# Macaron block on one core: GpSimd's rounding, subtraction and weight spreading cut into smaller instructions

## The reference, cut to what matters

```python
x = x + 0.5 * ffn(layernorm(x), ...)          # first FFN
x = x + attention(layernorm(x), Wq, .., memory_keys, memory_values)
x = x + 0.5 * ffn(layernorm(x), ...)          # second FFN, same weights

# ffn: 4096 tokens of width 128, 8 experts, the best 2 of each token, hidden width 176
scores = sigmoid(x @ gate_w.T); sel = top_k(scores + expert_bias, 2)
# routed: token times its score, bf16 products, square(relu(x @ up_e.T)) @ down_e.T, summed over the 2
# shared: square(relu(x @ shared_up.T)) @ shared_down.T, in fp32

# attention: 4096 keys and values of width 128, fp32
q = x @ Wq.T + bq
out = softmax(q @ memory_keys.T / sqrt(128)) @ memory_values @ Wo.T + bo
```

## Time and profile before

| | |
|---|---|
| median of three runs | 636.55 us (635.56 to 638.65) |
| profiled execution | 636.61 us, its span 634.8 us |
| TensorE clock granted | full in all of the span |
| PE busy | 599.1 us (94%) |
| DVE busy | 528.3 us (83%) |
| ACT busy | 454.0 us (72%) |
| POOL busy | 415.5 us (65%) |
| first FFN | about 0 to 111 us of the span |
| second FFN | about 544 us to the end |

### The profile page before, as it was taken

The page is one execution under the profiler, slowest core; times in us unless marked ns, Lnnn a source line. Parts: engine busy times, 40 slices in busy tenths (PEclk is TensorE's granted clock), DMA queues, the critical chain, the costliest instruction groups (busy, mean ns, idle before and its releaser), DMA issues.

```text
span 634.8 us, 10665 instructions
## 1 busy us (share of the span) xinstructions
PE 599.1 (94%) x3508; PEld 443.4 (70%) x3508; DVE 528.3 (83%) x913; ACT 454.0 (72%) x756; POOL 415.5 (65%) x484
## 2 busy tenths in 40 slices
PE   7799989899899999999999999999999999899987
PEld 3466656567677777777877778777787767566655
DVE  5899886988977978978887897897888858899884
ACT  3577776576777867767777776776877786488886
POOL 4868980564476865966768687596678887536520
PEclk9999999999999999999999999999999999999999
DMA  8012120425447274473744727446374460000001
GB/s 310 13 34 68 35 68 1 128 65 124 117 99 172 56 170 106 95 162 75 161 99 103 169 60 170 106 94 158 76 162 89 115 133 1 1 2 35 36 18 50
DMA packets 36118, 59.28 MB, mean 93 GB/s; under 512 B 9312, under 2 KB 9952, under 8 KB 35936
## 3 DMA queue, kind: packets, MB, share of 16 engines
q1 hardware_dynamic: 31808, 52.82, 33.9%
q10 hardware_dynamic: 3744, 4.74, 3.0%
q0 software_dynamic: 512, 1.05, 0.6%
HBM read 8.25 MB, written 2.10 MB: 16 GB/s over the span
## 4 chain that ended last, share of the span: by engine, by line
PE 57%; DVE 16%; POOL 10%; issue 9%; SPq 3%; ACT 3%; ACTq 0%; DMA 0%; POOLq 0%; DVEq 0%
PE banks L1501 7%; PE banks L1502 7%; PE banks L1503 7%; PE banks L1546 7%; PE banks L1548 7%; PE banks L1547 7%; PE banks L1525 4%; DVE bank_max L1218 4%; SPq L387 3%; DVE E L1213 3%; POOL xn L524 3%; DVE probsT L1100 2%; PE banks L1556 2%; PE banks L1358 2%; PE banks L1343 1%
## 5 line engine op out<-in xcount | busy, mean ns | idle before, releaser
L612 POOL TENSOR_TENSOR p_lo<-probsT,p_hi 128x768 fp32r<-128x768 f32 (+1 forms) x128 | 226.7, 1776 | 119.6 <-ACT p_hi L822 119.1
L1218 DVE TENSOR_REDUCE bank_max<-banks 128x1 f32<-128x1024 f32 x128 | 155.9, 1219 | 30.5 <-PE banks L1503 29.7
L822 ACT ACTIVATE p_hi<-probsT 128x768 fp32r<-128x768 f32 (+1 forms) x128 | 104.4, 816 | 28.2 <-PE banks L1548 24.4
L1501 PE MATMUL banks<-kv_lo,q_parts 128*128 128x512 f32 x256 | 111.6, 436 | 4.1 <-ACT E L847 1.8
L1213 DVE STREAM_TRANSPOSE E<-E 128x1024 f32<-128x1024 f32 x92 | 113.5, 1234 | 0.4
L1100 DVE SCALAR_TENSOR_TENSOR probsT<-banks,E 128x1024 bf16<-128x1024 f32 x80 | 96.0, 1218 | 20.9 <-PE banks L1343 19.6
L847 ACT ACTIVATE E<-banks,neg_max 128x1024 f32<-128x1024 f32 x92 | 102.4, 1113 | 10.4 <-DVE neg_max L1224 8.0
L1546 PE MATMUL banks<-p_hi,kv_lo 128*128 128x512 f32 x256 | 107.6, 420 | 1.4 <-issue 1.1
L720 ACT ACTIVATE probsT<-probsT 128x1024 bf16<-128x1024 bf16 x96 | 92.1, 981 | 17.9 <-DVE probsT L1100 14.8
L1548 PE MATMUL banks<-p_hi,kv_hi 128*128 128x512 f32 x256 | 102.3, 400 | 0.0
L1547 PE MATMUL banks<-p_lo,kv_hi 128*128 128x512 f32 x256 | 102.2, 399 | 0.0
(11 more groups left out here) (133 smaller groups left out, 935.5 us busy)
## 6 DMA issues: line engine op xcount, KB each, us to landing
probsT<-E SPq DMA_DIRECT2D x208, 128.0 KB, 2.4
probsT<-E SPq DMA_DIRECT2D x232, 64.0 KB, 2.0
probsT<-E ACTq DMA_DIRECT2D x72, 64.0 KB, 2.1
E<-in_keys_values SPq DMA_DIRECT2D x8, 512.0 KB, 3.5
out<-X SPq DMA_DIRECT2D x8, 256.0 KB, 2.0
X<-in_x SPq DMA_DIRECT2D x1, 1280.0 KB, 9.0
probsT<-E POOLq DMA_DIRECT2D x16, 64.0 KB, 2.4
X<-in_x SPq DMA_DIRECT2D x3, 256.0 KB, 5.3
```

What stands on the lines that cost most here:

```text
L612: pool.tensor_tensor(moved_part(p_lo, ring), moved_pair(ring // UP, ring % UP), moved_part(p_hi, ring).bitcast(fp32), ALU.subtract).then_i ...
L822: act.activation(moved_part(p_hi, ring), moved_pair(ring // UP, ring % UP), ACT.Copy).then_inc(moved_hi_done, 1)
L1218: dve.tensor_reduce(bank_max[:, i % 2, h:h + 1], score_pair(u, i, h).rearrange("p b n -> p (b n)"), AX.X, ALU.max).then_inc(bank_max_done, 1)
L1501: pe.matmul(bank, qh, kl, start=True, stop=False)
```

## The change

The rounding of a block becomes eight instructions of 128 columns instead of one of 1024. The subtraction becomes eight of 128 instead of four of 256. Each subtraction now waits for the rounding of its own columns and no longer for the whole block, though all eight roundings come first in the stream. The spreading of weights, in both FFNs, is done in parts of 16 weights by 16 copies, that is 256 columns. A pair of groups takes four instructions instead of one, the single groups 0 and 1 two instead of one. Group 8's weights are spread by VectorE (L1009) and do not change.

```diff
+KV_PARTS = 8
@@ spread_weights
-                pool.tensor_copy(wide_weights(G)[:, slots, :].rearrange("p s (m r) -> p (s m) r", r=ROWS),
-                                 weight[:, slots, :, :].rearrange("p s t e -> p (s t e)").unsqueeze(2)
-                                 .to_broadcast([P, T * E, ROWS])).then_inc(weights_spread, 1)
+                wide = wide_weights(G)[:, slots, :].rearrange("p s (m r) -> p (s m) r", r=ROWS)
+                narrow = weight[:, slots, :, :].rearrange("p s t e -> p (s t e)").unsqueeze(2)
+                for m in range(0, T * E, 2 * E):
+                    last = pool.tensor_copy(wide[:, m:m + 2 * E, :],
+                                            narrow[:, m:m + 2 * E, :].to_broadcast([P, 2 * E, ROWS]))
+                last.then_inc(weights_spread, 1)
@@ ffn, f == 0
-                        pool.tensor_copy(kv_hi[:, i, :], kv_stage[:, i % 2, :]).then_inc(kv_hi_done, 1)
-                        pool.wait_ge(kv_hi_done, i + 1)
-                        for a in range(0, KVW, KVW // 4):
-                            part = slice(a, a + KVW // 4)
+                        for a in range(KV_PARTS):
+                            part = bass.ds(a * KVW // KV_PARTS, KVW // KV_PARTS)
+                            pool.tensor_copy(kv_hi[:, i, part], kv_stage[:, i % 2, part]).then_inc(kv_hi_done, 1)
+                        for a in range(KV_PARTS):
+                            part = bass.ds(a * KVW // KV_PARTS, KVW // KV_PARTS)
+                            pool.wait_ge(kv_hi_done, i * KV_PARTS + a + 1)
                             last = pool.tensor_tensor(kv_lo[:, i, part], kv_stage[:, i % 2, part],
                                                       kv_hi[:, i, part].bitcast(fp32), ALU.subtract)
                         last.then_inc(kv_lo_done, 1)
```

## The result

The changed kernel takes 640.01 us (median of 14 runs, 637.76 to 642.70), the kernel before 637.22 (median of 14 on the same chip, 634.71 to 638.80). The ratio is 1.0049, 95% interval 1.0028 to 1.0070. The forecast was 638.0, with 635.0 to 641.8 as its range. So it is slower by 2.8 us, twice the +1.45 of the forecast, and at the edge of the 0.5% that counts as no change. The profiled execution took 637.90 us with a span of 635.7, against 636.61 and 634.8 before.

The account below looks back on a forecast made before the run. TensorE sets even iterations and waits for VectorE, stalled by GpSimd, in odd ones; the change makes GpSimd the bound. First FFN +0.55 and second +0.9 give +1.45 us, so 638.0 us, range 635.0 to 641.8.

Parts of the forecast that it names:

- Iteration 1: First FFN: VectorE's stalls fall from 0.90 to about 0.4 us, so GpSimd starts the pair's weights 0.5 us earlier.
- The last hand-over: First FFN, third pair: GpSimd starts at 83.7, TensorE turns the weights at 85.95 instead of 85.38 us.
- The first FFN's sum: The first FFN ends 0.55 us later, with a GpSimd cycle of 22.5 us instead of 21.47.
- Group 0's 0.12: First FFN, iteration 0: spreading group 0's weights in two parts takes 0.12 us longer, paid in full.
- The steps of VectorE: First FFN: a sign to look for, VectorE's routing steps all under 0.5 us.
- What VectorE wins: First FFN: shorter stalls win about 1.1 us in each of iterations 3 and 5, becoming waiting on TensorE for GpSimd.
- The fixed cost of an instruction: GpSimd blocks: 11 more instructions at about 0.12 to 0.14 us each, less a 0.08 gap, add 1.26 us a block.
- Second FFN: Three pairs spread later by 0.36, 0.36 and 0.17 us, +0.9 us in all, with nothing won against it.
- its own case: The whole kernel: the forecast itself, a time of 637.0 to 639.7 us, chance 0.48.
- Pieces dearer: Rival: pieces cost more than the line, a block grows by 2.06 us or more, 641.8 to 644.3 us; chance 0.20.
- GpSimd keeps up: Rival: blocks grow little, GpSimd stays off the path and VectorE's gain comes through, 633.6 to 635 us; chance 0.13.
- The two effects cancel: Rival: the weights' lateness is smaller and partly taken up in odd iterations, 636 to 637 us; chance 0.19.

Follow-up runs that it names:

- filler_long: The kernel before, with four GpSimd memsets of 1024 columns added behind each of the blocks 0 to 4; 645.21 us, ratio 1.0121.
- again: The changed kernel run once more without any edit; 642.01 us, ratio 1.0073 to the kernel before.
- moved_eighths_whole: The changed kernel with one-copy spreading and blocks reordered: block 0 behind iteration 1, block 1 behind 3, six behind 5; 634.48 us, ratio 0.9968 to before.
- spread_whole: The changed kernel with the spreading of before, one copy, so only the blocks are in eighths; 637.72 us, ratio 1.0003 to before.
- spread_eighths: The kernel before, its blocks unchanged, with the spreading in parts of 128 columns; 641.32 us, ratio 1.0068.
- casts_eighths: The kernel before with only the rounding in eighths, subtractions in quarters behind one wait, spreading whole; 636.98 us, ratio 1.0001.
- subtract_eighths: The kernel before with only the subtraction in eighths, rounding and spreading whole; 637.46 us, ratio 0.9997.
- moved: The kernel before with blocks reordered: block 0 behind iteration 1, block 1 behind 3, six behind 5, same instructions; 632.53 us, ratio 0.9935.
- filler: The kernel before, with two GpSimd memsets (1024 and 512 columns) added behind each of the blocks 0 to 4; 637.30 us, ratio 1.0004.
- moved_eighths: The changed kernel with blocks reordered: block 0 behind iteration 1, block 1 behind 3, six behind 5; 636.56 us, ratio 0.9985 to before.
- blocks_as_before: The changed kernel with the blocks of before, so only the spreading is in parts; 638.85 us, ratio 1.0032 to before.

## Why the prediction came out as it did

- **What bounds.** It said that GpSimd would become the bound of the cycle, with the pairs at 38.7, 61.2 and 83.7. They start at 38.67, 61.20 and 83.71, without idle time before the last two. `filler_long` shows that GpSimd's length then passes to TensorE. Right for the cycle and for the turning of iteration 3. Of the signs it named, TensorE's idle time before L1323 came in iteration 3. In iteration 5 it is 0.17 us at most, because there VectorE is the last to come, as shown above.
- **Size of a piece and of the cycle.** 457, 287 and 395 ns were forecast, 454, 292 and 398 measured. The casts overlap less, so a block is 5.28 us and not 5.16, +1.38 instead of +1.26. The cycle is still 22.5 as forecast, because the gap of 0.08 put before the waiting instruction didn't come and some hundredths were saved at the joints. That the two errors cancel is luck.
- **Iteration 1, the first term that was mis-sized.** VectorE's stalls there fell from 0.90 to about 0.3 us, more than the forecast's 0.4. But from the turning of weights to the pair's start it is 38.67 - 30.01 = 8.66 us against 8.93, so of the 0.6 won on stalls 0.27 arrived, where the forecast counted 0.5. The start at 38.67 hides that: this profile stands 0.18 us earlier at the first mark than the one of before, where the forecast had it 0.12 later.
- **The last hand-over, the second.** Turnings were forecast at 63.45 and 85.95 and came at 63.50 and 86.17. The last weights are ready at 83.71 + 0.78 + 1.42 = 85.91, and TensorE starts 0.26 us behind them, not 0.05. The forecast took the weights for what releases this turning. It hangs on VectorE, and that its time was hit to 0.2 us is luck, because the two come almost together. The 0.21 us in rows 1 and 3 were no hand-over either: TensorE came to both turnings straight from its own products, so they were slack. Where TensorE really waits for the weights it starts 0.10 to 0.11 us behind them (40.98 and 63.50).
- **The first FFN's sum.** Between its two marks the forecast stands for +0.43 (its +0.55 less the 0.12 of group 0, ahead of the first mark). Measured were +0.99, and +1.06 in `again`. The two terms above, 0.23 and 0.21, are most of the gap. The first hand-over adds 0.07 (40.98 - 38.67 = 2.31 us against 2.24), the rest is roundings. By beats the +0.99 is 0.94 in iteration 3, 0.11 in each of the iterations 2 and 4, and -0.19 in iteration 5. Group 0's 0.12 is there: TensorE idles 0.44 us for the weights at 16.02, and 0.31 before.
- **The steps of VectorE.** That none would be over 0.5 us was wrong. The routing's first step, which adds 1 to the exponentials (TENSOR_SCALAR), now meets the longer block:

```profile
31.18 0.28 DVE L1048 TENSOR_TENSOR route<-route,best 128x64 f32<-128x64 f32 x1
...
50.42 0.68 DVE L1074 TENSOR_SCALAR route<-probs 128x64 f32<-128x64 f32 x1
...
55.62 0.45 DVE L1055 TENSOR_TENSOR route<-route,best 128x64 f32<-128x64 f32 x1
...
58.02 0.40 DVE L1051 TENSOR_TENSOR route<-route,rank 128x64 f32<-128x64 f32 x1
```

  The first step of the routing (50.42) stands for 0.48 us, until the subtractions of that block end (47.70 + 3.35 = 51.05). Ahead of the turning at 63.50 GpSimd sets the pace and it should cost little. The same stand at 72.95 lies on VectorE's way to the turning at 86.17. In `moved_eighths_whole` such a stand, with what follows from it, costs 0.68 per odd beat.
- **What VectorE wins.** The forecast counted about 1.1 us less stalling in each of the iterations 3 and 5. In iteration 3 it is 0.3: the stalls are 0.48 + 0.23 + 0.13 + 0.18 + 0.15 = 1.17 us against 1.49, since each is shorter but five steps are held up instead of three. Over the first FFN they fell from 3.80 to 2.63 us. This term was much too large. It did not reach the sum, which let all of that gain turn into waiting for GpSimd.
- **The fixed cost of an instruction.** A block grew by 1.38 us for 11 more instructions, 0.125 us each. The estimate from the Trainium skill, GPSIMD Engine Reference, section "Instruction dispatch" (0.46 us a block at 50 cycles each) would have kept GpSimd off the path; no run bears it out.
- **Second FFN.** +0.9 was forecast, as 0.36 + 0.36 + 0.17, and +1.03 measured. TensorE's beats give 0.38, 0.36 and 0.29 for the three pairs, so the last one is the term that was too small. For the first pair TensorE turns the weights 0.20 and the tokens 0.33 us later than in the earlier trace rows. `spread_whole` takes all of it back and `spread_eighths` brings +2.58.
- **Around the span.** Costed at nothing; it is +0.35. This step was missing from the sum altogether.
- **The time.** 640.01 us lies above the 637.0 to 639.7 that the forecast gave to its own case. The whole series of runs stood higher by 0.67 (the kernel before at 637.22 and not 636.55), and the rest is the effect, +2.8 where +1.45 was forecast. The path was right in the main, and the sum about half of what came.
- **The rivals.** *Pieces dearer* is out at its bounds (a block of 5.96) but points in the right direction. *GpSimd keeps up* is out for the whole change, since the idle time before L540 is gone; for half of it, `casts_eighths` and `subtract_eighths`, it holds, and what VectorE was to win there did not show in the medians. *The two effects cancel* holds for the blocks alone (`spread_whole`, 1.0003) and falls for the change, because nothing stands against the spreading.

With group 0's 0.12 that is 0.12 + 0.99 + 1.03 + 0.35 = 2.5 us of the 2.8 between the medians. The rest is below what they resolve: the interval of the ratio is 2.7 us wide.

## What to carry to other kernels

Cutting a GpSimd instruction so that VectorE gets in more often pays for every piece, here 0.12 to 0.14 us, on the engine whose slack per cycle (1.94 us) must hold them all. Count the pieces against that slack first, and never cut the instruction that another engine waits for as a whole. At each hand-over look whether the engine behind it stood idle for it: a product that is ready 0.21 us ahead is slack, not a wait. Where the work has no consumer for a long time, taking it out of the contended stretch (`moved`, -4.6 us between the medians, of them 3.2 in the first FFN) is worth more than making it finer.

## What the runs showed of the chip that was not expected

**Small pieces do not always let VectorE in.** Two-input steps mostly got in at the next boundary, 0.06 to 0.08 us after it. One waited out the rest of a train of eight casts (1.48 us). The TENSOR_SCALAR step with one input from SBUF waited for the end of the train each time it met one of subtractions or memsets (0.68 us in after, in `moved_eighths_whole` and in `filler`, 2.88 in `filler_long`), even where GpSimd only wrote. But at 28.68 in after it met a single cast with a normalising instruction straight behind it, took 0.31 us and ended 0.05 us behind the cast. The Trainium skill, SBUF — State Buffer, section "Who interferes with whom", has `tensor_scalar` among the operations that can enter a two-port mode and says that whoever issues first keeps the shared pair for the whole instruction. It has a two-input VectorE instruction contend with a GpSimd instruction that reads SBUF, but not with one that only writes. The traces agree with both: the two-input steps that met memsets in `filler_long` kept their 0.22 us, as at 63.82. What they add is that the "whole instruction" can become a whole train. Why one step gets in at a boundary and another doesn't was not settled.

**The time around the span.** It is 2.15 to 2.18 us in the three kernels with both edits (after, again, `moved_eighths`) and 1.78 to 1.84 in the eleven others, each a median; every single execution of the three lies above 2.1 and every one of the others below 1.9. It isn't either edit alone. The three have the most instructions (592 of GpSimd, against 572 in `spread_whole` and `moved_eighths_whole` and 484 before), which is the only thing they share that I found; the cause is open.

**The clock in the middle of a kernel.** In three of the fourteen profiles (`spread_whole`, `blocks_as_before`, `subtract_eighths`) TensorE's granted clock falls to 0.50 for some 3 us behind its idle gaps at about 25 to 27 us. From turning to turning iteration 0 then took 15.63, 14.93 and 15.20 us, and 14.00 where the clock was full. `filler_long` has such a fall at 57 us, `subtract_eighths` a second one at 85, and four others one in the attention at about 160 to 167 us. The profiles of before and after have none inside their work, so the table's distances for them are free of it. Other executions are not: of the 23 of before that stood beside `again`, 8 had a mean granted clock of at least 0.999 and took 635.83 us on average, the 15 others 637.76. Of the 14 of after, 5 took 638.28 and 9 took 641.14. So such falls can move a median by some 2 us.

At full clock the change costs 638.28 - 635.83 = 2.45 us, from two series of runs, and the stages above add up to 2.5. For `moved_eighths` this matters most: 10 of its 12 executions were at full clock against 10 of 34 of before, and at full clock it is 0.55 us slower (636.33 against 635.78), though its ratio is 0.9985.
